# Layer 2 of a three-layer graph attention kernel: DMA transfers add pairs of probability tiles before their denominators are taken

## The reference

```
def _gat_layer(h, adj_mask, W_l, lw, lb, a):      # layers 1 and 2
    Wh = h @ W_l
    L1, L2 = (lw[:C], lw[C:])
    u = Wh @ L1 @ a
    v = Wh @ L2 @ a
    c = lb @ a
    e = jax.nn.leaky_relu(u + v.T + c, negative_slope=ALPHA)
    scores = jnp.where(adj_mask, e, NEG_INF)
    att = jax.nn.softmax(scores, axis=1)
    return jax.nn.elu(att @ Wh)
...
for i in range(GDEP):                             # GDEP = 2
    h = ALPHA * x + (1.0 - ALPHA) * _gat_layer(h, mask, W[i], lin_w[i], lin_b[i], attn[i])
    outs.append(h)
return jnp.concatenate(outs, axis=-1) @ mlp_w + mlp_b
```

## Time and profile before

| | |
|---|---|
| median of 3 runs | 3466.57 us |
| profiled execution, its own time | 3468.16 us |
| its span, first to last instruction | 3466.3 us |
| instructions | 57726 |
| PE busy | 3147.1 us, 91% of the span |
| DVE busy | 2870.2 us, 83% |
| ACT busy | 2269.7 us, 65% |
| POOL busy | 113.6 us, 3% |
| mean granted PE clock, share of full speed | 0.982 |
| strip rounds (L816), all layers | x4096 instruction records, 397.4 + 123.1 us |

### The profile page before, as it was taken

One profiled execution on the slowest core, in us unless ns is written; L12 is line 12 of the kernel. 1 busy time (PEld: TensorE's weight loads), 2 busy tenths in 40 slices (PEclk: granted clock), 3 DMA queues, 4 the chain that ended last, 5 costly groups with the idle time before them and its releaser, 6 DMA issues. The chain is left out here.

```text
span 3466.3 us, 57726 instructions
## 1 busy us (share of the span) xinstructions
PE 3147.1 (91%) x22637; PEld 1103.8 (32%) x22745; DVE 2870.2 (83%) x5292; ACT 2269.7 (65%) x3934; POOL 113.6 (3%) x138
## 2 busy tenths in 40 slices
PE   1479999999999999699999999997999999999998
PEld 0123333333333333233333333332333333333333
DVE  5468888888888875699999999986888888888886
ACT  0247766767677667477777777874666666666665
POOL 0000000000000000000000000000000000000000
PEclk9989999999999999799999999998999999999999
DMA  8899999999999971222222222212112111211200
GB/s 244 290 345 345 335 342 339 335 340 338 335 339 342 335 224 54 85 86 96 79 101 74 101 74 101 74 61 98 72 57 86 69 72 57 98 72 57 86 33 7
DMA packets 414114, 578.68 MB, mean 167 GB/s; under 512 B 294402, under 2 KB 315010, under 8 KB 389266
## 3 DMA queue, kind: packets, MB, share of 16 engines
q1 hardware_dynamic: 409458, 564.40, 50.5%
q0 software_dynamic: 4384, 10.59, 1.0%
HBM read 430.10 MB, written 77.69 MB: 146 GB/s over the span
## 5 line engine op out<-in xcount | busy, mean ns | idle before, releaser
L1178 DVE SCALAR_TENSOR_TENSOR eps<-ua,v8col,cb 128x512 f32<-128x512 f32 x2800 | 1966.9, 753 | 340.6 <-ACT prob L586 210.6
L586 ACT ACTIVATE prob<-eps,v2col 128x512 f32<-128x512 f32 x2560 | 1627.6, 689 | 662.2 <-PE eps L766 649.0
L807 PE MATMUL acc<-prob,feat 128*64 128x512 f32 x5120 | 1303.4, 605 | 6.4 <-ACT acc_s L594 6.4
L766 PE MATMUL eps<-nt,nbig 128*64 128x512 fp8e4 (+2 forms) x6642 | 987.4, 384 | 136.3 <-DVE eps L1178 128.7
L766 PEld LDWEIGHTS eps<-nt,nbig 128*64 128x64 bf16 (+2 forms) x6642 | 327.2, 103 | 987.3 <-DVE eps L1178 637.8
L807 PEld LDWEIGHTS acc<-prob,feat 128*64 128x64 f32 x5120 | 327.6, 137 | 397.5 <-issue 212.2
L586 ACT ACTIVATE mi<-eps,v2col 128x512 f32<-128x512 f32 x512 | 328.0, 686 | 149.8 <-PE eps L766 146.3
L1008 DVE TENSOR_SCALAR mi<-stage 128x1024 uint8<-128x1024 int32 x512 | 351.9, 689 | 69.6 <-DMA stage<-in_adj_dram 69.3
L816 PE MATMUL den<-prob,ones 128*32 128x512 f32 x3072 | 397.4, 605 | 0.0
L807 PE MATMUL acc<-mi,feat 128*64 128x512 f32 x1024 | 264.5, 597 | 0.0
L1017 DVE TENSOR_SCALAR edges<-nt 128x2048 int32<-128x2048 int32 x192 | 234.1, 1219 | 30.9 <-PE misc L777 16.4
(11 more groups left out here) (164 smaller groups left out, 1285.0 us busy)
## 6 DMA issues: line engine op xcount, KB each, us to landing
stage<-in_adj_dram SPq DMA_DIRECT2D x512, 512.0 KB, 6.7
nt<-nt_d SPq DMA_DIRECT2D x128, 1024.0 KB, 5.1
nt_d<-nt SPq DMA_DIRECT2D x64, 1024.0 KB, 7.2
ub<-u_d SPq DMA_DIRECT2D x48, 256.0 KB, 5.3
xy_d<-xin POOLq DMA_DIRECT2D x32, 256.0 KB, 3.2
xin<-xy_d SPq DMA_DIRECT2D x32, 256.0 KB, 2.9
nt<-mi SPq DMA_TRANSPOSE x256, 7.4
xin<-in_x_dram SPq DMA_DIRECT2D x16, 128.0 KB, 6.3
```

Of the source, the lines that this page charges most:

```text
L586: nc.scalar.activation(weights(l, j), eps[:, j % ES, :], ACT.Exp, bias=v2col[:, j:j + 1]).then_inc(s_p, 1)
L766: mm = nc.tensor.matmul(et[c:c + cols, :], nbig[:, c:c + cols], edge, start=False, stop=True, skip_group_check=True, tile_position=(0, c))
L807: mm = nc.tensor.matmul(acc[h:h + C, :], feat[:, l % 2, j, 0:C], weights(l, j), start=(k == 0), stop=(k == NT // 2 - 1))
L1178: dv.scalar_tensor_tensor(eps[:, j % ES, :], ua[:, par, :], v8col[:, j:j + 1], cb[:, par, :], ALU.add, ALU.max).then_inc(s_fill, 1)
```

## The change

In layer 2 the 64 tiles of a block make eight groups of eight, g = 0 to 7. For g = 0 to 5 POOL now issues two transfers per group with an adding destination (`accum_op=ALU.add`). One adds tiles 2 and 3 of the group onto tiles 0 and 1, the other tiles 6 and 7 onto 4 and 5, in place, once `main` has used them. PE then takes the denominators of such a group in one strip round over tiles 0, 1, 4 and 5 instead of two rounds over eight tiles. It does so twelve tiles later than before (t = 8(g+1)+15 instead of 8(g+1)+3). Groups 6 and 7 keep two rounds at their old place; group 6 comes before group 5. Since tiles live longer, there are 24 places instead of 16; the third set lies over `stage`, which only layer 0 uses.

```diff
+ADDED = (0, 1, 2, 3, 4, 5)
+ADDLAG = 15
+DEN_ORDER = (0, 1, 2, 3, 4, 6, 5, 7)
+ADDS = 6
+RSTD_AT = 3
-SLOTS = (TS, TS, 2 * TS)
+SLOTS = (TS, TS, 3 * TS)
...
+            def add_probs(b, g):
+                for h in range(2):
+                    pool.wait_ge(s_main, group(2, b, 4 * g + 2 * h + 1) + 1)
+                    buf, o = places(b, DEN * g + QUAD * h)
+                    nc.gpsimd.dma_start(buf[:, o:o + 2, :], buf[:, o + 2:o + 4, :], accum_op=ALU.add).then_inc(
+                        added(b, g, h)[0], 16)
...
+            for b in range(NB):
+                for g in range(NT // DEN):
+                    if g == RSTD_AT and b > 0:
+                        last_rstd(b - 1)
+                    if g in ADDED:
+                        add_probs(b, g)
+                    if g == RSTD_AT and b > 0:
+                        result(b - 1)
...
-                    elif b or j >= 2 * TS:
-                        act.wait_ge(s_den, b * (NT // DEN) + j // DEN - 1)
+                    elif b or j >= 3 * TS:
+                        c, g = divmod(b * (NT // DEN) + j // DEN - 3, NT // DEN)
+                        act.wait_ge(s_den, den_done(c, g))
...
-            def two_quads(b, g):
-                denominators(2, b, 2 * g)
-                denominators(2, b, 2 * g + 1).then_inc(s_den, 1)
+            def eight_probs(b, g):
+                if g == DEN_ORDER[0]:
+                    pe.wait_ge(s_dene, den_blocks(2, b))
+                if g in ADDED:
+                    for h in range(2):
+                        pe.wait_ge(*added(b, g, h))
+                rounds = ((0, 1, 4, 5),) if g in ADDED else ((0, 1, 2, 3), (4, 5, 6, 7))
+                for n, tiles in enumerate(rounds):
+                    for i, j in enumerate(tiles):
+                        mm = nc.tensor.matmul(den[32 * i:32 * i + 32, :], ones[:, 0:32], weights(2, b, DEN * g + j),
+                                              start=(g == DEN_ORDER[0] and n == 0),
+                                              stop=(g == DEN_ORDER[-1] and n == len(rounds) - 1))
+                mm.then_inc(s_den, 1)
...
-                        if l == 2 and t % DEN == DLAG:
-                            g = t // DEN - 1
-                            if g >= 0:
-                                two_quads(b, g)
-                            elif tail:
-                                two_quads(b - 1, NT // DEN + g)
+                        for g in DEN_ORDER if l == 2 else ():
+                            at = DEN * (g + 1) + (ADDLAG if g in ADDED else DLAG)
+                            if t == at:
+                                eight_probs(b, g)
+                            elif t == at - NT and tail:
+                                eight_probs(b - 1, g)
```

More of the change, by code:

```diff
@@ L200, in build @@
         den = ps("den", [P, BI])
+        rest = stage[:, 0:TS * BI // CW, :].rearrange("p s w -> p (s w)").bitcast(F32).rearrange(
+            "p (s w) -> p s w", w=BI)
         more = mi[:, :, :].rearrange("p s w -> p (s w)").bitcast(F32).rearrange("p (s w) -> p s w", w=BI)
@@ L256, in build @@
         s_den = sem("probs_in_denominators")
+        s_two = [sem(f"probs_added_by_two{i}") for i in range(ADDS)]
         s_setup = sem("setup_steps")
@@ L308, in landed, with places, weights, added @@
             return s_mload[b % 2 * MV + m], 16 * ((l - 1) * (NB // 2) + b // 2 + 1)
-        def weights(l, j):
-            n = j % SLOTS[l]
-            return prob[:, n, :] if n < TS else more[:, n - TS, :]
+        def places(b, j):
+            q, o = divmod((b * NT + j) % SLOTS[2], TS)
+            return (prob[:, :, :], more, rest)[q], o
+        def weights(l, b, j):
+            if l < 2:
+                return prob[:, j % SLOTS[l], :]
+            buf, o = places(b, j)
+            return buf[:, o, :]
+        def added(b, g, h):
+            n = 2 * (b * len(ADDED) + ADDED.index(g)) + h
+            return s_two[n % ADDS], 16 * (n // ADDS + 1)
+        def den_done(b, g):
+            return b * (NT // DEN) + DEN_ORDER.index(g) + 1
         def freed(l, b, j):
@@ L533, in tail, with last_rstd, result @@
                     nc.gpsimd.dma_start(xy_v[l, b], xin[:, :, :]).then_inc(s_x1, 16)
[L534 to L540, removed]
+            def last_rstd(b):
+                pool.wait_ge(s_mom2, b + 1)
+                nc.gpsimd.tensor_tensor(rstd[:, :], mom2[:, :], half[:, :], ALU.pow).then_inc(s_rstd2, 1)
+            def result(b):
+                pool.wait_ge(s_fin, b + 1)
+                nc.gpsimd.dma_start(out_v[b], pj[:, :, :]).then_inc(s_out, 16)
+            def add_probs(b, g):
[4 more added lines that the diff above has]
+                        added(b, g, h)[0], 16)
+            for l in range(2):
                 for b in range(NB):
                     tail(l, b)
+            for b in range(NB):
[6 more added lines that the diff above has]
+                        result(b - 1)
+            last_rstd(NB - 1)
+            result(NB - 1)
         @block.scalar
@@ L582, in probs @@
                         act.wait_ge(s_main, group(2, 0, 0))
-                    elif b or j >= 2 * TS:
-                        act.wait_ge(s_den, b * (NT // DEN) + j // DEN - 1)
+                    elif b or j >= 3 * TS:
+                        c, g = divmod(b * (NT // DEN) + j // DEN - 3, NT // DEN)
+                        act.wait_ge(s_den, den_done(c, g))
                 act.wait_ge(s_z, tile(l, b, j) + 1)
-                nc.scalar.activation(weights(l, j), eps[:, j % ES, :], ACT.Exp,
+                nc.scalar.activation(weights(l, b, j), eps[:, j % ES, :], ACT.Exp,
                                      bias=v2col[:, j:j + 1]).then_inc(s_p, 1)
@@ L806, in main @@
                         pe.wait_ge(s_acce, blk(l, b))
-                    mm = nc.tensor.matmul(acc[h:h + C, :], feat[:, l % 2, j, 0:C], weights(l, j),
+                    mm = nc.tensor.matmul(acc[h:h + C, :], feat[:, l % 2, j, 0:C], weights(l, b, j),
                                           start=(k == 0), stop=(k == NT // 2 - 1))
@@ L815, in denominators @@
                 for i in range(QUAD):
[L816 removed]
+                    mm = nc.tensor.matmul(den[32 * i:32 * i + 32, :], ones[:, 0:32], weights(l, b, QUAD * k + i),
                                           start=(k == 0), stop=(k == NT // QUAD - 1))
@@ L961, in _ @@
                 if l == 2:
-                    two_quads(NB - 1, NT // DEN - 1)
+                    for g in DEN_ORDER:
+                        if DEN * (g + 1) + (ADDLAG if g in ADDED else DLAG) >= NT:
+                            eight_probs(NB - 1, g)
                 for t in range(NT):
```

## The result

The changed kernel took 3443.92 us (median of 4 runs, 3442.64 to 3447.01) beside 3466.74 for the kernel before: a ratio of 0.9935, 95% interval 0.9922 to 0.9947. It is 23 us faster, where 52 were forecast. The direction and most of the mechanism were right; the gain is less than half of the one forecast.

What follows compares the result with a forecast made beforehand. PE was taken to bound layer 2; 5.55 us of rounds removed a block, less 0.65 and 1.8 us of waits for DVE, left 3.1, 52 us in all, so 3415 us; own range 3398 to 3434, overall 3376 to 3458.

Steps and rivals of the forecast that it cites:

- What bounds the kernel: Layer 2: PE sets the pace, busy 398 of 400 us; DVE needs 56.7 of a block's 67.37 us.
- What is removed: Layer 2's strip rounds: six of 16 go, at 0.925 us each, 5.55 us a block.
- What DVE and PE lose against each other: PE waits for DVE's bursts: 0.65 us at tiles 21 and 23, 1.8 us at t = 52 to 55.
- What is added: Twelve adding transfers a block, 2.46 us each, hidden beside PE and landing before their rounds.
- it fits by 0.4 us: Group 3's round at t = 47: transfers done 12.3 us after the variances end, round due at 12.7.
- The sum: A block takes 64.3 us, 3.1 less; 52 us saved over the kernel.
- The other costs at nothing: POOL's issues, 12 by 0.78 us, in an idle queue; DVE starts not lengthened; edge-instruction lockout at most 0.8 us each.
- (a): Rival: all 5.55 us a block gained, since DVE's lead is larger or bursts fall behind rounds; 3378 us, chance 0.12.
- (b): Rival: adds take 3.5 us, group 3 lands late beside mask loads, PE waits 1.7 us a block; 3444 us, chance 0.12.
- (c): Rival: DMA engines bound layer 2, kernel slower; 3565 us at 5 us an add, 3890 at 6.7; chance 0.18.

Runs made afterwards that it cites:

- the run with the features later: The changed kernel with layer 2's tail_features on DVE at t = 23 instead of t = 20: 3438.67 us, ratio 0.9918.
- the four moves: The changed kernel with POOL's power between group 3's transfers, tail_features at t = 23, head at t = 52, group 3's round behind the fold: 3405.57 us.

## Why the prediction was wrong

**What bounds the kernel.** Right: PE set the pace, and fewer rounds made it faster.

**What is removed.** The term was mis-sized. I took half of a double round, 0.925 us. Its rows had no lone round in them, and the interruption that stays was not in the half. A lone round takes 0.99 to 1.00, so by the price of 0.86 halving six double rounds saves 5.2 us a block, not 5.55. Two of the six saved less, since they stood beside counts of edges. In the kernel before:

```profile
2617.07 0.41 PE L766 MATMUL eps<-nt,nbig 128*64 128x512 fp8e4 x2 [0.17 <-DVE eps L1178]
...
2618.26 1.92 PE L816 MATMUL den<-prob,ones 128*32 128x512 f32 x16
2620.00 1.91 PE L777 MATMUL misc<-edges,oneh 128*32 128x512 fp8e4 x32
```

This double round took 1.74 us (2618.26 to 2620.00), not 1.98. Summed from the starts of the masks around them, the six double rounds had taken 11.2 us and the six lone ones take 6.2: 5.0 us saved. The extra waits of PE cost nothing that shows, since a lone round takes 0.99 us without them and 0.99 to 1.00 with them.

**What DVE and PE lose against each other.** Right in place and nearly in size. Tile 21 waited 0.60 us (0.55 forecast). Tiles 52, 53 and 55 show 0.47 + 0.66 + 0.26 = 1.4 us of idle time. By the starts of rows both cost a little more. From tile 20 to the round of t = 23 it takes 3.50 us (2584.72 to 2588.22) and 2.69 in the run with the features later (2583.68 to 2586.37): 0.8 where 0.65 was forecast. From the mask behind the fold to that of t = 56 it takes 8.42, and 7.48 in the block shown of the run with the fold first (2609.26 to 2616.74), 0.99 of which is its wait for a transfer: 1.9 where 1.8 was forecast. Moving either burst, or the fold ahead of the round, changed the time.

**What is added.** This is the step that failed, in the words "it fits by 0.4 us". The price of a transfer was nearly right: twelve took 49.7% of the 16 engines over 65 us of one block, 2.7 us each (the store of the result counted in) against 2.46 forecast, and where nobody waited for them they cost nothing. The landing of group 3 was not. I summed the bytes of two loads and two transfers in series to 12.3 us after the variances. The round was released 15.1 us after them (2599.67 to 2614.80), and PE had reached it at 13.7, later than my 12.7. So the estimate was short by 2.8 us, and its margin was smaller than that. A sum at full rate is the earliest time at which everything can be done, and I used it as the expected one, with PE behind it. That the collision with the loads is the cause is shown twice, by moving them and by issuing one transfer ahead of them. With the loads moved the kernel takes 3429.45 us: the waits were half of the 29 us missing, and the terms above are most of the other half. How its 2.8 us divide between the late start of POOL's packets behind SP's and the share that the next transfers and the store took, no run separates.

**The sum.** A block came out 2.06 us longer than forecast by the mean (66.33 against 64.27). Of this the rounds are 0.6, the waits for group 3 1.1 (15.4 us of idle time over 14 blocks), the bursts 0.3 and the slower clock 0.1. Against them goes 0.2 for tile 43: PE waited for it before too (0.17 us of idle time; 1.74 us from the mask of t = 42 at 2616.52 to the round at 2618.26), and the same step takes 1.53 now (2607.22 to 2608.75). Some 0.1 to 0.2 is left without a name.

**The other costs at nothing.** POOL's issues (0.86 us each instead of 0.78) cost nothing by themselves: with the transfers on unused memory the kernel before kept its time. DVE lost nothing either: score starts had a median of 754 ns with those transfers and without, and the edge instructions 1218 ns in the changed kernel and 1219 before. POOL did lose beside an edge instruction. The first pair of rows is from the changed kernel, the second from the one with the four moves:

```profile
2604.95 1.22 DVE L1074 TENSOR_SCALAR edges<-nt 128x2048 int32<-128x2048 int32 x1
2605.29 1.00 POOL L570 DMA_DIRECT2D mi<-mi  x1 [0.60 <-PE acc L851]
```

```profile
2598.36 1.58 POOL L572 DMA_DIRECT2D mi<-mi  x1
2598.61 1.22 DVE L1081 TENSOR_SCALAR edges<-nt 128x2048 int32<-128x2048 int32 x1
```

The issue of group 4's first transfer took 1.00 us in nearly every block of the changed kernel and up to 1.59 with the four moves, where most others took 0.85. With the four moves no round waited for a transfer, so there it cost nothing. The rule of "SBUF — State Buffer", section "Who interferes with whom", of the Trainium skill says that GpSimd is starved while it writes descriptors beside such a DVE instruction, and these rows agree, with up to 0.74 us an issue. It did not meet group 3, whose issues end before the edge instructions of t = 40 and 41 begin.

**The rivals.** Of (a), that all is gained, there was no sign. Rival (b), group 3 late beside the loads, is what happened, at its place and for want of its margin; I gave it 0.12. Its price for a transfer, 3.5 us, was not needed: at 2.7 the landing was late all the same. That its time of 3444 us is the measured one is luck. It had 1.7 us of waiting a block where 1.1 was found, and the rounds and bursts, 0.9 a block short, and a last block that gained 4.1 us instead of 1.4, made up for it. Of (c), DMA as the bound, nothing was seen up to a share of 0.83.

## What to carry to other kernels

When a compute engine is made to wait for a transfer, set the transfer's landing against everything else that is issued at that moment; a margin of a few tenths of a microsecond on a sum of bytes at full rate is no margin, and the rival that it fails deserves the larger chance. Price a removed piece from a row in which it stands alone, with the interruption that remains. And order the steps inside one slot so that what another engine waits for (here the fold) stands ahead of what waits itself (the round): exchanging two rows gained 21 us, nearly as much as the 23 of the whole change.

## What the runs showed of the hardware that was not expected

An adding transfer of 512 KB from one place of SBUF to another costs the DMA engines about 2.7 us of all 16, a little over the time of twice its bytes at 427 GB/s (2.46). With DMA busy 0.71 of layer 2 the kernel before kept its time, and at 0.83 the score starts still had a median of 753 ns. Issued right behind two loads of 1 MB, two such transfers landed after 10.2 and 12.9 us instead of 5.7. A transfer's issue on POOL took up to 1.59 us instead of 0.85 beside a DVE edge instruction, which itself kept its 1.22 us. An idle stretch of 3.22 us on PE, in an otherwise dense stream, was followed by some 6 us at 1.2 GHz, which cost 1.8 us beside the wait. A strip round put between two pairs costs PE 0.13 us beside its own 0.99.
